# Two-layer recurrent block: expert tiles ordered by chunk, and the first scan chunk prepared between the last expert tiles

## The reference, cut to what matters

```python
xn = layernorm(x)
# layer 0, mixer: h_t = f_t * h_(t-1) + z_t along each sequence, in bf16
xr = rmsnorm(xn); og = silu(xr @ Wga.T) * (xr @ Wgb.T)
f = sigmoid(xr @ Wf.T + b); z = (xr @ Wz.T) * sigmoid(xr @ Wzg.T)
s = (og * scan(f, z)) @ Wout.T + b_out + xn
# layer 0, experts: top 1 of 4, hidden 1024
e = argmax(softmax(xn @ Wr + br)); w = its probability
g = silu(w * ((silu(xn @ Wg[e]) * (xn @ Wu[e])) @ Wd[e]))
x1 = x + s * g; xn = layernorm(x1)
# layer 1: selective scan
xc = silu(conv4(xn @ W_in_x)); z = xn @ W_in_z
dt, B, C = split(xc @ W_x.T); delta = softplus(dt @ W_dt.T + b_dt)
state = exp(delta * A) * state + (delta * xc) * B     # 16 states, 512 channels
y = (sum over states of state * C + D * xc) * silu(z)
out = x1 + (y @ W_out.T + b) * silu(xn @ bw.T + bias)
```

## Time and profile before

| | us |
|---|---|
| median of 3 runs | 1448.37 |
| lowest, highest | 1448.21, 1448.73 |
| the profiled execution | 1449.39 |
| its span, first to last instruction | 1447.6 |
| PE busy in the span | 1372.4 (95%) |
| DVE, ACT, POOL busy | 1006.2, 878.8, 904.9 |
| last expert product ends, by the timeline | 585.5 |
| first unit of the scan starts | 629.5 |

### The profile page before, as it was taken

One profiled execution on the slowest core, in us unless ns is written; L12 is line 12 of the kernel. 1 busy time (PEld: TensorE's weight loads), 2 busy tenths in 40 slices (PEclk: granted clock), 3 DMA queues, 4 the chain that ended last, 5 costly groups with the idle time before them and its releaser, 6 DMA issues.

```text
span 1447.6 us, 23480 instructions
## 1 busy us (share of the span) xinstructions
PE 1372.4 (95%) x8622; PEld 1079.9 (75%) x8652; DVE 1006.2 (70%) x1342; ACT 878.8 (61%) x1457; POOL 904.9 (63%) x578
## 2 busy tenths in 40 slices
PE   7999999999999999879799999999999999999988
PEld 4445469999999999447667867777777778678777
DVE  7755542232232232468898998999999989989896
ACT  4211121111111111288999999999989999999983
POOL 4222211222222222149999999999999999999994
PEclk9999999999999999999999999999999999999999
DMA  9921136766676764113342352533524433523542
GB/s 299 404 91 44 58 124 239 253 263 234 254 262 244 260 259 164 41 40 93 89 102 74 84 121 75 124 95 93 127 67 110 113 92 89 132 74 87 133 98 63
DMA packets 57761, 205.17 MB, mean 142 GB/s; under 512 B 6575, under 2 KB 32815, under 8 KB 48822
## 3 DMA queue, kind: packets, MB, share of 16 engines
q1 hardware_dynamic: 42358, 146.55, 29.1%
q0 software_dynamic: 15296, 57.19, 17.2%
HBM read 141.78 MB, written 31.00 MB: 119 GB/s over the span
## 4 chain that ended last, share of the span: by engine, by line
PE 58%; POOL 27%; issue 6%; DVE 6%; DMA 2%; ACT 1%; SPq 0%; POOLq 0%; DVEq 0%; ACTq 0%
POOL hst L705 20%; PE bank L1546 17%; PE bank L1559 8%; PE bank L1491 7%; PE bank L1734 5%; PE bank L1621 3%; PE bank L1754 3%; POOL xpad L665 3%; PE bank L1613 2%; POOL dbuT L687 2%; PE bank L1651 2%; PE bank L1632 2%; PE bank L1742 2%; DVE hst L1391 2%; DMA hst<-hst 1%
## 5 line engine op out<-in xcount | busy, mean ns | idle before, releaser
L1391 DVE TENSOR_TENSOR_SCAN hst<-dA,carry,bank 128x512 f32<-128x512 f32 x512 | 631.3, 1267 | 66.7 <-PE bank L1734 43.6
L705 POOL TENSOR_TENSOR hst<-hst,c_bc 128x2048 f32<-128x2048 f32 x127 | 581.9, 4611 | 17.1 <-POOL carry L700 3.9
L933 ACT ACTIVATE dA<-delta,negA 128x512 f32<-128x512 f32 x512 | 354.9, 714 | 9.2 <-DVE hst L1391 9.0
L1734 PEld LDWEIGHTS bank<-ident,dbuT 128*128 128x128 f32 x2048 | 241.8, 141 | 150.2 <-issue 69.3
L1734 PE MATMUL bank<-ident,dbuT 128*128 128x128 f32 x2048 | 311.1, 276 | 36.2 <-DVE hst L1391 29.4
L922 ACT ACTIVATE dbuT<-duT,bT 128x512 f32<-128x512 f32 x382 | 269.8, 713 | 5.8 <-PE bank L1734 5.8
L1546 PEld LDWEIGHTS bank<-f_sb,w_gu 128*128 128x128 f32 x2240 | 255.5, 192 | 2.7 <-ACT f_sb L769 1.0
L1546 PE MATMUL bank<-f_sb,w_gu 128*128 128x128 f32 x2240 | 256.0, 275 | 0.7 <-ACT f_sb L769 0.7
L1754 PE MATMUL bank<-ident,hst 128*128 128x128 f32 x1520 | 210.0, 274 | 4.6 <-POOL hst L705 3.0
L640 POOL TENSOR_TENSOR x_sb<-x_sb,neg_half 128x1 f32<-128x1 f32 x35 | 23.0, 656 | 260.6 <-DVE x_sb L1224 260.6
L1754 PEld LDWEIGHTS bank<-ident,hst 128*128 128x128 f32 x1520 | 174.7, 142 | 7.5 <-POOL hst L705 4.9
(11 more groups left out here) (206 smaller groups left out, 1709.3 us busy)
## 6 DMA issues: line engine op xcount, KB each, us to landing
w_gu<-in_w_gu SPq DMA_DIRECT2D x35, 2048.0 KB
c_bc<-c_rows SPq DMA_DIRECT2D x64, 512.0 KB, 4.2
hst<-hst POOLq DMA_DIRECT2D x31, 1024.0 KB, 9.0
sorted_x<-sg_a SPq DMA_DIRECT2D x12, 387.0 KB, 11.6
x_sb<-sorted_x SPq DMA_DIRECT2D x35, 129.0 KB
x_sb<-in_x SPq DMA_DIRECT2D x8, 512.0 KB, 7.7
w_d<-in_w_d SPq DMA_DIRECT2D x1, 4096.0 KB, 20.2
x_mix<-x_sb SPq DMA_DIRECT2D x1, 4096.0 KB, 29.9
```

Source lines behind the costliest of these rows:

```text
L705: pool.tensor_tensor(h[:], h[:], c, ALU.mult).then_inc(hc_ready, 1)
L933: act.activation(dA[:, at % DA_BUFS, :], delta[q % B][:, d, :], ACT.Exp, scale=negA[:, d, n:n + 1]).then_inc(dA_ready, 1)
L1391: v.tensor_tensor_scan(h[:, d, :], dA[:, at % DA_BUFS, :], bank[4 + u % 2][:], carry1[q % B][:, n, d:d + 1], ALU.mult, ALU.add).then_inc(s ...
L1734: ins = pe.transpose(bank[4 + u % 2][:, i * P:(i + 1) * P], dbuT[(DS * q + n) % DBU_BUFS][:, i, d * P:(d + 1) * P], ident[:])
```

## The change

Chunks get a storage order, `STORED` = 0, 2, 4, 1, 3, 6, 5, 7: first the five chunks that the scan takes first (0 to 4), sequence 0 before sequence 1, then the last three. The input tiles are laid in this order on the host, and the mixer runs through them in it, with a carry for each sequence. `place_rows` counts each expert's rows twice, in the first 20 tiles and in all 32, and gives places so that expert tiles 0 to 22 hold all rows of chunks 0 to 4. The rows of chunks 5 to 7 first fill the places left in the last early tile of their expert, and the others go to the tiles behind, up to the last 12. The expert list `eid` goes through the four experts twice.

With that, the rows of chunk 0 are complete when tile 22 is scattered. The meeting on `layer0_done` and the 12 idle products are gone. On each engine a function `prologue(j, k)` is called at up to four places of expert tile j, with k = 0 behind the first half, 1 behind the second, 2 behind the turn or the residual, 3 behind the output product, and holds the pieces of chunk 0's preparation. SP loads chunk 0's rows at j = 24 and chunk 1's at j = 27. The banks for the preparation are 5 and 6, which the experts don't use, where it had seven before. The delta of chunk 0 is made in two steps on DVE (`biased`, `first_delta`), the first of which frees the bank ahead of softplus. The residual and normed row of the last tiles are laid behind the first three units of the scan on DVE (`last_tiles`). Buffers that shared memory are laid out anew so that what is written early lies over nothing that is still read.

```diff
+A_CHUNKS = 5
+EARLY_SLOTS = SLOTS - TPC * (CHUNKS - A_CHUNKS)
+STORED = sorted(range(CHUNKS), key=lambda c: (c >= A_CHUNKS, c % B, c // B))
+FIRST_CLAIMS = {"X0": 5, "X1": 6, "X2": 5, "X3": 6, "XN0": 5, "XN1": 6, "DT": 5, "DL0": 5, "DL1": 6, "DL2": 5, "DL3": 6,
+                "BC": 5, "BT": 6, "DUT0": 5, "DUT1": 6, "DUT2": 5, "DUT3": 6}
...
@@ SP @@
+            def load_first():
+                wait_scattered(sp, EARLY_SLOTS)
+                for half in range(2):
...
+                    sp.dma_start(x_ld[:, lo:lo + TPC // 2, :], x1_xn_t[:, rows, D:2 * D]).then_inc(xn2_first[half], 16)
             for j in range(SLOTS):
                 if j + 2 < SLOTS:
                     sp.wait_ge(up_ready, 2 * j + 2)
                     load_up(j + 2)
+                if j == EARLY_SLOTS + 1:
+                    load_first()
+                if j == EARLY_SLOTS + 4:
+                    load_xn(1)
-            sp.sem_inc(layer0_done, 1)
-            sp.wait_ge(layer0_done, 5)
             store_c(0)
+            sp.wait_ge(down_ready, SLOTS)
...
@@ POOL @@
+            def prologue(j):
+                if j == 32:
+                    make_du(-1, 0)
+                    make_du(-1, 1)
+                    make_du(-1, 2)
...
+                if EARLY_SLOTS <= j < SLOTS:
+                    prologue(j)
...
@@ ACT @@
+                if (j, k) == (31, 2):
+                    act.preload_act_table_set("natural_log_exp_and_others")
+                    for d in range(DB):
+                        exp_capped(d, DB + d)
+                    for d in range(DB):
+                        ln_capped(d, DB + d + 1)
+                    act.wait_ge(a_pre, 2)
+                    for d in range(DB):
+                        decay(0, d)
...
@@ DVE, place_rows @@
+                for last, n in ((A_TILES - 1, n_a), (TILES - 1, n_b)):
+                    then(v.tensor_tensor(cmp, cum[:, last, :].unsqueeze(2).broadcast_to([P, NE, TILES]),
+                                         steps128.unsqueeze(1).broadcast_to([P, NE, TILES]), ALU.is_gt))
+                    then(v.tensor_reduce(n, cmp, AX_X, ALU.add))
+                then(v.tensor_tensor(n_b, n_b, n_a, ALU.subtract))
+                then(v.tensor_tensor_scan(end_a, rs[:, 3, 0:NE], n_a, 0.0, ALU.mult, ALU.add))
+                then(v.tensor_tensor_scan(end_b, rs[:, 3, 0:NE], n_b, end_a[:, NE - 1:NE], ALU.mult, ALU.add))
+                then(v.tensor_tensor(start_a, end_a, n_a, ALU.subtract))
+                then(v.tensor_tensor(start_b, end_b, n_b, ALU.subtract))
+                then(v.tensor_tensor(jump, start_b, end_a, ALU.subtract))
+                then(v.tensor_scalar(jump, jump, float(P), None, ALU.mult))
+                then(v.tensor_scalar(lim, n_a, float(P), None, ALU.mult))
...
+                then(v.tensor_tensor(tot, cum, per_expert(lim), ALU.is_ge))
+                then(v.tensor_tensor(tot, tot, per_expert(jump), ALU.mult))
+                then(v.tensor_tensor(cum, cum, tot, ALU.add))
...
@@ DVE, the scan @@
+            def last_tiles(u):
+                if u == 0:
+                    normed_row(SLOTS - 2)
+                if u == 1:
+                    residual(SLOTS - 1)
+                if u == 2:
+                    normed_row(SLOTS - 1)
+                if u == DVE_DELTA[0] - 1:
+                    wait_scattered(v, SLOTS)
...
@@ PE @@
-            pe.sem_inc(layer0_done, 1)
-            for i in range(IDLE_PRODUCTS):
-                pe.matmul(bank[0][:], w_in[:, 0, 0:P], w_in[:, 0, 0:CH], start=True, stop=True)
-            pe.wait_ge(layer0_done, 5)
+                if (j, k) == (34, 3):
+                    for d in range(DB):
+                        wait_freed(pe, -1, f"DUT{d}")
+                    pe.wait_ge(hid_ready, 2 * SLOTS)
+                    spread(0, 0)
+                    spread(0, 1)
...
             down(SLOTS - 1, e)
+            spread(0, 2)
+            pe.wait_ge(ye_ready, SLOTS)
```

More of the change, by code:

```diff
@@ new lines, in _ @@
+            turn_in(0)
+            gate(0, 0)
+            gate(0, 1)
+            turn_in(1)
+            for j in range(1, SLOTS):
+                gate(j, 0)
+                prologue(j, 0)
+                if j == BW_TILE:
+                    act.wait_ge(bw_turned, 1)
+                    act.copy(bwT[:], bank[7][:].rearrange("p (k o) -> p k o", k=KB)).then_inc(bwT_ready, 1)
+                gate(j, 1)
+                prologue(j, 1)
+                if j + 1 < SLOTS:
+                    turn_in(j + 1)
+                prologue(j, 2)
+                silu_out(j - 1)
+                prologue(j, 3)
@@ L1116, in place_rows @@
+                then(v.scalar_tensor_tensor(cum, per_expert(start_a), float(P), cum, ALU.mult, ALU.add))
                 then(v.tensor_tensor(cum, cum, oh, ALU.mult))
@@ new lines, in first_pieces, with biased @@
+            def first_pieces():
+                wait_freed(v, -1, "DUT3")
+                wait_freed(v, -1, "BT")
+                for i in range(TPC - FIRST_PIECES, TPC):
+                    v.tensor_scalar(dbuT[0][:, i, :], duT[0][:, i, :], bT[0][:, i, 0:1], None,
+                                    ALU.mult).then_inc(dbuT_first, 1)
+            def biased(d):
+                wait_full(v, -1, f"DL{d}")
+                v.wait_ge(soft_step, d + 1)
+                is_freed(v.tensor_scalar(delta[0][:, d, :], place(-1, f"DL{d}")[:], cols1[:, d, KC + 1:KC + 2], None,
+                                         ALU.add), -1, f"DL{d}")
@@ new lines, in _ @@
+            hidden(0, 0)
+            hidden(0, 1)
+            binary_weights()
+            for j in range(1, SLOTS):
+                hidden(j, 0)
+                prologue(j, 0)
+                hidden(j, 1)
+                prologue(j, 1)
+                residual(j - 1)
+                prologue(j, 2)
+                if j >= 2 and j != EARLY_SLOTS + 1:
+                    normed_row(j - 2)
+                if j == EARLY_SLOTS:
+                    normed_row(j - 1)
+                prologue(j, 3)
@@ L1757, in add_up, with turn_first @@
                 ins.then_inc(y_added, 1)
-            pe.wait_ge(scan_set, 8)
-            for half in range(2):
+            def turn_first(half):
                 pe.wait_ge(xn2_first[half], 16)
@@ new lines, in _ @@
+            e = expert(0)
+            up(0, 0)
+            up(0, 1)
+            turn_in(1)
+            for j in range(1, SLOTS):
+                before, e = e, expert(j)
+                up(j, 0)
+                prologue(j, 0)
+                if j == BW_TILE:
+                    turn_bw()
+                up(j, 1)
+                prologue(j, 1)
+                if j + 1 < SLOTS:
+                    turn_in(j + 1)
+                prologue(j, 2)
+                down(j - 1, before)
+                prologue(j, 3)
@@ L1793, in _ @@
                     if u + 1 < UNITS:
-                        spread(q, u + 1)
+                        if unit(q, u) > 1:
+                            spread(q, u + 1)
                     elif q + 1 < CHUNKS:
@@ L1880, in spread @@
         return np.broadcast_to(r, (P, *r.shape))
+    tiles = [c % B * TPB + c // B * TPC + i for c in STORED for i in range(TPC)]
     wt = [rows(np.asarray(w).T) for w in (L0_attn_Wf_w, L0_attn_Wzg_w, L0_attn_Wz_w, L0_attn_Wga_w, L0_attn_Wgb_w)]
@@ L1917 @@
     got = r.results[0]["out_0"]
-    return np.ascontiguousarray(np.swapaxes(got, 0, 1)).reshape(B, T, D)
+    return np.ascontiguousarray(np.swapaxes(got[:, np.argsort(tiles)], 0, 1)).reshape(B, T, D)
```

440 lines of the change are left out of this document (230 added, 210 removed).

## The result

The changed kernel takes 1427.33 us (median of 4 runs, 1425.69 to 1428.33), against 1448.55 us for the kernel before on the same chip (4 runs, 1448.21 to 1449.40). The ratio is 0.9852, 95% interval 0.9834 to 0.9869. In the profiled executions it is 1426.5 us of span against 1447.6, so 21.1 us less, where 18.0 were predicted.

A forecast was written before the change was run, and what follows sets the result against it. PE was taken to bound the expert stage, and a chain of short steps between engines the stretch before the scan. -45.1 + 24.1 - 0.8 + 0.5 + 3.3 = -18.0 gave 1430.4 us, range 1425 to 1437.5.

The forecast's parts named there:

- boundary: From last expert product to the scan's fourth unit: 50.4 us shrink to 5.3, -45.1.
- work in the tiles: Chunk 0's preparation laid onto PE in expert tiles 26 to 34: +24.1 us, bounds 23.1 and 26.4.
- small terms: Expert tiles: spreads cover the wait before the last output product, -0.8; one new PE wait in tile 29, +0.5.
- place_rows: Mixer chunk 0: 12 more DVE instructions make PE wait about 3.0, the rest at the next chunk; +3.3 us.
- behind the start of the scan: Behind the fourth unit no engine's list changes, so the shift goes to the end unchanged.
- 40 records: Tiles 26 to 34: 20 products of 512 columns on PE, 0.436 us a record, 17.4 us.
- 44 transposes: Tiles 26 to 34 on PE: normed rows 1.0 + 1.4, delta times x and B 3.1, two spreads 1.2 us.
- ACT's block: Tile 31: table loads, exp, ln and decays in one piece, 10.9 us, margin 2 us, so 0 cost.
- rival 1: Tiles 27 to 34: new hand-over waits replace the old one; PE stands about 6, 1436.4, at most +10.9; chance 0.17.
- rival 2: Start of the scan takes part back through late C, POOL or lower clock; 1434 us; chance 0.07.
- rival 3: Tiles 26 to 34: PE's clock falls; 50 us at the lower level gives 1455 us; chance 0.02.
- rival 4: Chunk 0's rows come late, PE stands in tile 26; with all gain lost 1451.7 us; chance 0.01.

The follow-up runs named there:

- The filler: Changed kernel with seven more exp of 128x512 in ACT's block of tile 31; 1427.72 us, ratio 0.9861.
- the first experiment: The changed kernel measured again with no edit; 1426.30 us, ratio 0.9851.
- e2_place_late: Changed kernel with all but the counting and rank steps of place_rows, and chunk 1's rows, behind mixer chunk 0's second half; 1423.00 us, again 1424.17.
- the filler on PE: Changed kernel with four more f32 products of 512 columns behind the first half of tile 30; 1430.80 us, ratio 0.9877.

## Why the prediction was right, step by step

The direction, the mechanism and the range held; the time lay 3.1 us below the 1430.4. The signed parts, in the profiled executions, as predicted and as measured: boundary -45.1 and -45.7, work in the tiles with its small terms +23.8 and +22.0, place_rows +3.3 and +3.7, and 0 and -1.1 behind the start of the scan.

**The boundary.** 50.4 us were to become 5.3; they became 4.7, so -45.7 and not -45.1. The path went as the prediction had it: DVE in order, SP's load of C issued at T (611.22), POOL not late. DVE began at T - 1.95 where T - 1.9 was predicted, and took 6.7 us up to the fourth unit and not 7.2: from the start of a scan to the start of the next operation are 1.19 us (609.25 to 610.44) where its own duration reads 1.27, which I had added up.

**PE's work in the tiles.** Here is the largest error. +23.8 was predicted with the two small terms, +22.0 came (123.8 - 101.8). The 40 records were right (groups of four take 1.72, so 17.2). The 44 transposes were too dear: I had 0.15 to 0.156 each, from groups with slow clock and waits in them (287 and 327 ns). Back to back, eight take 0.87, 0.11 each, so 4.8 for all where 6.7 stood in the sum; 17.2 + 4.8 - 0.8 + 0.7 gives 21.9. The lower bound that I had worked out from the fastest group, 0.13, was itself too high: the row of a group reads longer than the group's share of a full list. Eight transposes at 494.57 read 1.04 us, and the next group starts 0.88 us after them, at 495.45.

**Small terms.** The wait of 0.76 was covered, and the experiment that moved the spreads shows by what. The one wait that the walk had found, 0.5 in tile 29, is there with 0.68. No other came.

**ACT's block.** 10.9 with a margin of 2 was predicted, 10.1 with 2.7 measured: four ln and four decays take 2.55 each where 2.9 stood in the sum. The Trainium skill (ScalarE: Activation LUTs, What ACT_TABLE_LOAD costs) adds 1.38 of drain to every switch of tables; by that, as an estimate, the two loads would have cost 2.8 more, the whole margin. The trace agrees with its 1.28 for the load and shows no drain: the first load starts 0.02 us behind the copy's end, the second 0.01 behind the decays', and the operation behind each starts 0.01 or 0.02 us after it. The filler gives the margin again as 5.27 - 2.66 = 2.6.

**place_rows.** +3.3 predicted. The size is right by the medians of the order alone (3.3) but not for the reason in full. The sum of the twelve instructions was good: from DVE's first gated half to its second are 61.78 - 50.70 = 11.08 us, where the kernel before has 58.78 - 51.12 = 7.66, so 3.4. PE stands 3.4 to 3.6, not 3.0. At the next chunk the prediction let the rest of the 3.3 come on top of the old wait of 0.78; in fact that wait goes, since PE comes later. That makes 2.7 in all. The twelve products behind the wait then run at the lower clock in some executions, 1.3 more in the profile of the changed kernel, and the prediction had no step for that. So 3.57 + 1.3 - 0.78 = 4.1 were given in this profile, of which 0.4 came back because this execution's mixer ran that much earlier from the start (DVE's first gated half at 50.70 and not 51.12): 84.31 - 80.59 = 3.7 at chunk 1. That the forecast of 3.3 meets the 3.3 of the medians is luck in part: one term was too large, and one was missing.

**The start of the scan and behind.** -45.7 + 22.0 + 4.1 - 0.4 = -20.0, the measured shift of POOL's first product. The prediction let this shift go to the end unchanged; 1.1 us more come. They are a sum of larger pieces (the table under the first experiment, first profile): 0.8 up to 1358, in small steps; -1.2 at 1362.5, where POOL waits for DVE behind a stretch of low clock (1342.97 in the changed kernel's own time):

```profile
1342.97 4.55 POOL L731 TENSOR_TENSOR hst<-hst,c_bc 128x2048 f32<-128x2048 f32 x1 [0.84 <-DVE hst L1497]
```

then +1.2 up to 1424.8, where the kernel before has its own stretch of low clock and the changed one none; and 0.3 to 0.4 behind it. Of the small steps, the 0.3 in chunk 1 stands where POOL had stood 0.46 ahead of a product:

```profile
720.24 4.56 POOL L705 TENSOR_TENSOR hst<-hst,c_bc 128x2048 f32<-128x2048 f32 x1 [0.46 <-POOL carry L700]
```

The row names POOL's own copy, which had long been done; what it really waited for stays open.

**The rivals.** New waits in the tiles (rival 1): one, of 0.7. The start of the scan giving a part back (rival 2): none, the fourth unit is at T + 4.7, and the stretch of low clock lies as far behind the first product with C as before. Rows of chunk 0 too late (rival 4): PE doesn't stand in tile 26. The clock (rival 3) stays at 1.00 in the tiles; it fell where the prediction did not look, behind PE's wait in the mixer. (The prediction gives these tiles 115 us. By its own numbers they are 101.8 + 23.8 = 125.6; the chance given to this rival doesn't hang on it.)

## What to carry to other kernels

Work laid into a stage that one engine bounds costs its duration on that engine and nothing on the others: count it with durations taken from the inside of full lists, and look for a wait it can cover, since two short steps between two products, the second of which waited for ACT's step behind the first, were worth 2.3 us here. A reordering pays for its tables too: look where the longer table-making stands in an in-order list, and move it behind the step that the bounding engine waits for. Judge differences of 1 or 2 us by the distance between two events inside the stage, since totals also carry stretches of low clock that can fall otherwise from one execution to the next: here 1 to 1.7 us each, as much as some of the effects looked for.

## What the runs showed of the hardware

Short stretches in which the clock is at the lower of its two levels (1.2 GHz in place of 2.4) cost by what falls into them. In every profile one follows the start of the scan, where PE stands 0.7 to 1.3 us before several units. In the changed kernel it begins 7.7 us behind the first product with C, at 625.3; PE's work fills the slice to the brim:

```profile
625.00:630.00 5.00, 5.00 (x15) 2.52 (x14) 4.36 (x5) 4.44 (x9) 4.69 (x2) 0.66 0.00 0
1320.00:1325.00 5.00, 4.34 (x24) 4.10 (x25) 3.67 (x4) 5.00 (x9) 5.00 (x3) 0.66 0.94 151
```

In e2_place_late it begins 1.5 us behind that product, at 615.8, where PE still waits a fifth of the time:

```profile
615.00:620.00 5.00, 4.00 (x14) 2.51 (x14) 5.00 (x6) 4.97 (x10) 3.90 (x1) 0.66 0.00 2
1320.00:1325.00 5.00, 5.00 (x47) 4.85 (x45) 4.66 (x5) 5.00 (x9) 5.00 (x4) 1.00 0.59 207
```

Between POOL's first and ninth product with C e2_place_late gains 1.7 us on the changed kernel (3.2 becomes 4.9) without a difference in the two lists there. The ten profiles fall into two groups. Where the stretch begins 6.7 to 7.7 us behind the first product (the kernel before, the order alone, the changed kernel twice, the spreads moved), the ninth comes 57.9 to 58.1 us behind it. Where it begins 1.4 to 2.3 us behind it (e2_place_late twice, the kernel with one wait less, both fillers), it is 56.4. Both profiles of the changed kernel are in the first group and both of e2_place_late in the second, so this stretch was not seen to move between executions of one program. What puts it in one place or the other was not settled.

The second rows show a stretch near the end that does come and go. The changed kernel has it at 1321.6 in both profiles, e2_place_late has none in the first and has it at 1316.3 in the second. Five of the profiles have it (these three, the kernel with one wait less and the filler on PE), and all five lose 1.0 to 1.2 us against the kernel before at the product that stands there at 1362.5; in the other four profiles compared with it nothing is lost there. The kernel before has its own at 1415:

```profile
1415.00:1420.00 5.00, 4.45 (x23) 4.21 (x24) 3.88 (x4) 3.04 (x5) 5.00 (x2) 0.66 0.31 105
```

The kernel with the order alone has one there too and shifts by nothing against it; the other eight profiles have none and all gain 1.1 to 1.2 us there. So two executions of one program can differ by more than the 0.6 us of the changed kernel's two: those of e2_place_late are up to 1.4 us apart behind 1362.5.

Behind a wait of 3.4 to 3.6 us in the mixer, the next twelve bf16 products took 1.47 us in two profiles and 1.9 to 2.8 in four. In these six the products began within 0.7 us of each other (62.54 to 63.20), the long ones both ahead of and behind the short; what decides was not settled. Nor was it tried whether idle products in that wait would hold the clock.
